# Attention with row maxima over 1024 keys at once, two banks for the transposed scores, and projection pieces in every step

## What is computed

```
x = x + attention(layernorm(x))
    q, k, v = proj(w_q), proj(w_k), proj(w_v)       # heads of 16 channels
    scores = q k^T / sqrt(16)                       # 1024 x 1024 for each of 64 (batch, head)
    out = softmax(scores) v
    out @ w_o^T
x = x + ffn(layernorm(x))                           # 512 -> 1376 (gate, up) -> 512, int4 / int8 rounding
```

## Time and profile before

| | us |
|---|---|
| median of 3 runs | 1142.4 |
| lowest and highest run | 1142.07, 1145.83 |
| the profiled execution, its own time | 1141.39 |
| its span | 1139.6 |
| PE busy | 1051.8 (92%) |
| DVE busy | 884.5 (78%) |
| ACT (ScalarE) busy | 738.2 (65%) |
| POOL (GpSimd) busy | 143.3 (13%) |
| ramp, first score to first transposed score | 66.4 to 137.2 |
| superunits 1 to 7, to the last value sum of each | 137.2 to 815.3 |
| superunit 8 | 815.3 to 900.9 |

### The profile page before, as it was taken

One profiled execution on the slowest core, in us unless ns is written; L12 is line 12 of the kernel. 1 busy time (PEld: TensorE's weight loads), 2 busy tenths in 40 slices (PEclk: granted clock), 3 DMA queues, 4 the chain that ended last, 5 costly groups with the idle time before them and its releaser, 6 DMA issues.

```text
span 1139.6 us, 18560 instructions
## 1 busy us (share of the span) xinstructions
PE 1051.8 (92%) x6882; PEld 354.3 (31%) x6882; DVE 884.5 (78%) x1573; ACT 738.2 (65%) x885; POOL 143.3 (13%) x282
## 2 busy tenths in 40 slices
PE   4889999999999999999999999999998669888886
PEld 2333222222222222222222222222222235444543
DVE  3265588988988897898888889889997267788874
ACT  4631277766777776776677677667778536656664
POOL 2200011011101201201110110111000021111210
PEclk9889999999999999999999999999999979999998
DMA  9430013102202300230220121022253251111110
GB/s 349 153 86 1 1 31 78 33 20 66 58 18 66 66 11 20 66 65 10 76 57 13 35 73 41 20 66 57 96 154 85 62 152 37 39 37 37 37 46 28
DMA packets 43862, 69.63 MB, mean 61 GB/s; under 512 B 3334, under 2 KB 21766, under 8 KB 43526
## 3 DMA queue, kind: packets, MB, share of 16 engines
q1 hardware_dynamic: 43782, 68.56, 21.6%
HBM read 46.99 MB, written 21.23 MB: 60 GB/s over the span
## 4 chain that ended last, share of the span: by engine, by line
PE 64%; DVE 12%; ACT 5%; issue 5%; DMA 5%; POOL 2%; SPq 1%; DVEq 0%; POOLq 0%; ACTq 0%
PE ps L360 20%; PE ps L312 17%; PE ps L297 10%; PE ps L341 8%; PE ps L275 4%; DVE mx L765 3%; PE ps L421 2%; ACT PB L571 2%; DMA QK<-parts_d 2%; DVE hm L860 2%; POOL rstd L1027 1%; DMA parts_d<-spl 1%; PE ps L443 1%; DVE bst L808 1%; DVE PB L806 1%
## 5 line engine op out<-in xcount | busy, mean ns | idle before, releaser
L765 DVE TENSOR_REDUCE mx<-ps 128x1 f32<-128x512 f32 x1024 | 653.3, 685 | 122.6 <-PE ps L312 116.8
L571 ACT ACTIVATE PB<-ps 128x1024 f32<-128x1024 f32 x512 | 522.5, 1024 | 196.5 <-PE ps L341 191.2
L312 PE MATMUL ps<-QK 48*128 48x512 f16 x1024 | 354.6, 385 | 11.4 <-DVE mx L765 8.2
L360 PE MATMUL ps<-PB,Vg 128*32 128x256 f32 (+1 forms) x3192 | 303.2, 451 | 8.7 <-ACT PB L571 4.6
L341 PE MATMUL ps<-QK 50*128 50x512 f16 x1024 | 300.4, 382 | 1.2 <-DMA QK<-nmT 1.1
L312 PEld LDWEIGHTS ps<-QK 48*128 48x128 f16 x1024 | 92.4, 92 | 431.3 <-DVE mx L765 379.6
L297 PE MATMUL ps<-XV,wqk 128*128 128x512 f32 x256 | 144.4, 656 | 0.0
L360 PEld LDWEIGHTS ps<-PB,Vg 128*32 128x32 f32 x3192 | 63.5, 107 | 110.9 <-issue 97.6
L421 PE MATMUL ps<-tu,Vg 128*128 128x344 bf16 x256 | 49.1, 315 | 24.6 <-DVE XV L849 24.6
L275 PE MATMUL ps<-wv,XV 128*128 128x512 f32 x128 | 69.4, 649 | 0.0
L399 PE MATMUL ps<-wo,XV 128*128 128x512 f32 x128 | 61.1, 622 | 6.0 <-DVE PB L806 5.2
(11 more groups left out here) (117 smaller groups left out, 657.7 us busy)
## 6 DMA issues: line engine op xcount, KB each, us to landing
parts_d<-spl SPq DMA_DIRECT2D x64, 128.0 KB
QK<-parts_d SPq DMA_DIRECT2D x32, 256.0 KB, 5.1
att_d<-OS SPq DMA_DIRECT2D x32, 256.0 KB
PB<-x SPq DMA_DIRECT2D x28, 256.0 KB, 2.9
QK<-parts_d SPq DMA_DIRECT2D x32, 128.0 KB, 4.7
XV<-att_d SPq DMA_DIRECT2D x2, 2048.0 KB, 8.4
QK<-rden_d SPq DMA_DIRECT2D x8, 512.0 KB, 7.8
out<-PB SPq DMA_DIRECT2D x16, 256.0 KB, 2.0
```

Source lines behind the costliest of these rows:

```text
L312: nc.tensor.matmul(ps[:, 4 + at % 2, :], QK[rows, sup % 2, 2 * set_ + p, 0, half * HALF + qt * P:half * HALF + (qt + 1) * P], QK[rows, sup ...
L360: last = nc.tensor.matmul(ps[32 * h:32 * h + 32, 6, part * n:part * n + n], Vg[:, set_, kt, h, :], PB[:, step % 2, h, part * n:part * n + ...
L571: nc.scalar.activation(PB[:, step % 2, 2 * pair:2 * pair + 2, :], ps[:, 2 * pair:2 * pair + 2, :], ACT.Exp, scale=exp_reg).then_inc(probs, 1)
L765: nc.vector.tensor_reduce(mx[:, unit % 2, qt * 4 + head, kh:kh + 1], ps[:, 4 + at % 2, :], AX.X, ALU.max)\
```

## The change

- A maximum is taken over 1024 keys in one instruction: an item is now two score matmuls into two neighbouring banks (banks 0 and 1, or 2 and 3) and one reduction of 128 x 1024, negated. A unit has 16 items in place of 32, a step two in place of four; the joining reduction and its buffer are gone.
- Transposed scores have two banks (4 and 5). Each head's matmul is followed by its own exponential of 512 columns, so a step has four exponentials in place of two. A transposed-score matmul waits for the exponential of the matmul before the last.
- PB has three buffers, in turn over all 256 steps.
- Jobs are numbered 0 to 31, k ahead of q, and run one job per unit: steps 0 to 6 of each unit carry one whole matmul and then six halves of 256 columns, step 7 none. Five jobs run ahead of the value projection in place of four, and the loop does 27 in place of 28.
- The value sum is always one piece, at the end of the step.
- In the ramp an item (two score matmuls) follows every second value matmul.
- The DMAs that stack q and k are cut into k, first half of q and second half of q, each with its own semaphore.

```diff
         def step_items(step):
-
             found = []
-            for j in range(4):
-                n = (step + AHEAD) * 4 + j
-                found.append((n // 128, n % 128 // 32, n % 32))
+            for j in range(2):
+                n = (step + AHEAD) * 2 + j
+                found.append((n // (4 * UNIT_ITEMS), n % (4 * UNIT_ITEMS) // UNIT_ITEMS, n % UNIT_ITEMS))
             return found
...
+        def job_in(sup, step):
+
+            n = 4 * sup + 5 + step // KEYT
+            return n if n < JOBS else None
...
-            last = nc.tensor.matmul(ps[:, job_bank(sup, job), :], wqk[:, qk, k, :], xT(region, k, half * HALF, HALF),
-                                    start=(k == 0), stop=(k == KT - 1))
-            if k == KT - 1:
+            last = nc.tensor.matmul(ps[:, job_bank(n), col:col + cols], wqk[:, qk, k, :],
+                                    xT(region, k, half * HALF + col, cols),
+                                    start=(k == 0 and col == 0), stop=(k == KT - 1 and col + cols == HALF))
+            if k == KT - 1 and col + cols == HALF:
                 last.then_inc(job_psum, 1)
...
-            if sup > 0 or step > 0:
-
-                pe.wait_ge(probs, sup * (2 * STEPS) + (2 * step + p - 1))
-            for side in range(2):
-                rows = slice(side * SIDE, side * SIDE + AUG)
-                last = nc.tensor.matmul(ps[:, 2 * p + side, :],
-                                        QK[rows, sup % 2, 2 * set_ + p, 1, kt * P:(kt + 1) * P],
-                                        QK[rows, sup % 2, 2 * set_ + p, 0, half * HALF:(half + 1) * HALF],
-                                        start=True, stop=True)
-            last.then_inc(st_psum, 1)
+                    pe.wait_ge(v_copy, TILES)
+            if n >= 2:
+                pe.wait_ge(probs, n - 1)
+            rows = slice(side * SIDE, side * SIDE + AUG)
+            nc.tensor.matmul(ps[:, 4 + i % 2, :],
+                             QK[rows, sup % 2, 2 * set_ + p, 1, kt * P:(kt + 1) * P],
+                             QK[rows, sup % 2, 2 * set_ + p, 0, half * HALF:(half + 1) * HALF],
+                             start=True, stop=True).then_inc(st_psum, 1)
...
             for step in range(STEPS):
-                jobs = not last and step < 16
-                item(step, 0)
+                job, r = job_in(sup, step), step % KEYT
+                item(step, 0, 0)
                 pe_scoresT(pe, sup, step, 0)
-                item(step, 1)
+                item(step, 0, 1)
+                pe_scoresT(pe, sup, step, 1)
+                if job and r == 0:
+                    pe_job(pe, job, 0)
+                elif job and r < 7:
+                    pe_job(pe, job, (r + 1) // 2, (r - 1) % 2 * (HALF // 2), HALF // 2)
+                item(step, 1, 0)
+                pe_scoresT(pe, sup, step, 2)
+                item(step, 1, 1)
+                pe_scoresT(pe, sup, step, 3)
                 if step > 0:
-                    pe_av(pe, sup, step - 1, 0, 1 if jobs else 2)
-                item(step, 2)
-                pe_scoresT(pe, sup, step, 1)
-                item(step, 3)
-                if jobs:
-                    pe_job(pe, sup + 1, region, step // 4, step % 4)
-                elif step > 0:
-                    pe_av(pe, sup, step - 1, 1, 2)
+                    pe_av(pe, sup, step - 1)
...
-                    if t >= RAMP_TILE and item < 4 * AHEAD:
-                        pe_scores(pe, 0, item // 32, item % 32)
+                    if t >= RAMP_TILE and k % 2 == 1:
+                        for kh in range(2):
+                            pe_scores(pe, 0, item // UNIT_ITEMS, item % UNIT_ITEMS, kh)
                         item += 1
...
-            nc.scalar.activation(PB[:, step % 2, 2 * pair:2 * pair + 2, :], ps[:, 2 * pair:2 * pair + 2, :],
+            nc.scalar.activation(PB[:, at % 3, 2 * (i % 2) + i // 2, :], ps[:, 4 + i % 2, :],
                                  ACT.Exp, scale=exp_reg).then_inc(probs, 1)
...
                 act_exp(act, sup, step, 0)
                 act_exp(act, sup, step, 1)
-                if step % KEYT == 0 and step > 0:
+                if step % KEYT == 1 and step > 1:
                     act_sums(act, sup, step // KEYT - 1)
-                if not last and step < 16 and step % 4 == 3:
-                    act_job(act, sup + 1, step // 4)
+                if step % KEYT == 7 and job_in(sup, step):
+                    act_job(act, job_in(sup, step))
+                act_exp(act, sup, step, 2)
+                act_exp(act, sup, step, 3)
                 if last and step in (12, 14, 16, 18):
                     act_abs(act, 2, (step - 12) // 2)
...
-            nc.vector.tensor_reduce(mx[:, unit % 2, qt * 4 + head, kh:kh + 1], ps[:, 4 + at % 2, :], AX.X, ALU.max)\
-                .then_inc(s_used, 1)
...
+            nc.vector.tensor_reduce(nm[:, unit % 2, idx:idx + 1], slot_of(at).rearrange("p a n -> p (a n)"), AX.X, ALU.max,
+                                    negate=True).then_inc(s_used, 1)
```

More of the change, by code:

```diff
@@ L1056, in _ @@
             g.tensor_tensor(rnorm[:], sqtot[:], expo[:, 0:2], ALU.pow).then_inc(wn_pow, 1)
[L1057 to L1058 removed]
+            for job in range(5):
+                pool_split_job(pool, job)
             rstds(2)
```

296 lines of the change are left out of this document (160 added, 136 removed).

## The result

The changed kernel is 0.8% slower: median 1148.95 us of 14 runs (1146.65 to 1158.33) against 1141.48 of 14 runs of the kernel before on the same chip, a ratio of 1.0076 with a 95% interval of 1.0057 to 1.0096. The forecast was 1135.5. The profiled execution took 1147.72 us, with a span of 1145.9.

The account below looks back on a forecast made before the run. PE was taken to bound steps with a job, DVE those without. Superunits -8.7, last superunit +10.9 and ramp -9.3 gave -7.1 on 1141.39, so 1134.3; the median stands 1.0 above, forecast 1135.5 us, range 1122 to 1160.

Parts of the forecast that it names:

- The maxima: Reductions over 1024 keys on DVE: 1.16 us each, 2.3 a step in place of 2.5; DVE no longer sets the pace.
- The ring: Each step: first transposed score (T0), its exponential (E0), the second exponential, fourth transposed score (T3), value sum, next T0; 2.88 us.
- The first rival: Exponentials in the ring don't overlap, each starting when the one before ends: +27 us, 1162 us; chance 0.2.
- The superunits: The six changed superunits take 95.8 us each for 97.05; with the first superunit and a saved job, -8.7 us.
- The ramp: Before the first transposed score: paired scores -6.8 us, with shorter waits, clock and a fifth early job together -9.3.
- the fifth job's 3.4: In the ramp: a fifth job ahead of the value projection adds four f32 matmuls, +3.4 us.
- The last superunit: It has no jobs, so the ring costs there: 96.6 us for 85.66, +10.9.
- rival two: The clock still falls in the ramp: +3.4 us, 1139 us; chance 0.2.
- T0: First of a step's four transposed scores on PE; from its start to E0's start 0.43 us.
- E0: First of a step's four exponentials on ACT, taken from T0; the second starts 0.48 to 0.49 us after it.
- T3: Fourth transposed score of a step on PE, waiting for the second exponential; from its start to the value sum 0.32 us.
- the fixed cost of a short exponential: Skill page's 0.57 us per 512-column exponential, against 0.48 between starts; as start to start, ring 0.09 longer.

Follow-up runs that it names:

- experiment 3: Changed kernel with the value sum between the second and third transposed score and the job's piece at the step's end; 1202.7 us, one run.
- experiment 4: Changed kernel with the value sum over only 256 of its 512 queries, half that work left out; 1114.0 us, one run.
- experiment 9: Changed kernel with the value sum in two pieces of 256 queries in the last superunit only; 1146.00 us, 1.0045 of the kernel before.
- Experiment 6: Kernel before with one edit, ramp scores in pairs after every second value matmul; 1131.70 us, 0.9917 of the kernel before.
- experiment 10: Changed kernel with three transposed-score banks from step 24 of superunit 6, four from step 21 of the last; 1123.71 us, 0.9835 of the kernel before.
- experiment 1: Changed kernel with four extra unread score matmuls in each of the last eleven steps; 1138.10 us, 0.9968 of the kernel before.
- experiment 7: Changed kernel with the value sum in two pieces throughout and ACT's copy of the sums ahead of the step's first exponential; 1186.74 us, 1.0412.
- experiment 2: Changed kernel with a third bank for transposed scores in the last superunit; 1131.15 us, 0.9908 of the kernel before.
- experiment 5: Kernel before with each 1024-column exponential cut into two of 512, all four transposed-score banks kept; 1145.91 us, 1.0026 of the kernel before.
- experiment 8: Experiment 7 with three transposed-score banks from the last superunit's first step and four from its step 21; 1191.6 us, uneven.
- experiment 11: Experiment 10 with experiment 9's edit, the value sum in two pieces in the last superunit; 1144.92 us, 1.0029 of the kernel before.
- experiment 12: Experiment 1 with experiment 9's edit, the value sum in two pieces in the last superunit; 1134.62 us, 0.9929 of the kernel before.

## Why the prediction was wrong

- **The maxima** were right: 1.22 us each, DVE no longer the pace.
- **The ring** was right to 0.01 us, with every link: 2.88 to 2.89 in steps with a half job piece and in steps of the last superunit. Experiments 3, 4 and 9 changed a link and got the step that the sum of the links gives. The first rival fell: exponentials of 0.597 start about 0.49 apart, two of them in 1.09:

```profile
311.11 1.09 ACT L593 ACTIVATE PB<-ps 128x512 f32<-128x512 f32 x2 [0.63 <-PE ps L366]
```

- **The superunits** were right in kind, 0.45 us too low each (96.25 for 95.8). The steps at a unit's edge took 3.09 + 3.29 + 3.15 = 9.53 for 9.46 computed; the rest was not traced further.
- **The ramp**: -8.9 for -9.3. Experiment 6 confirms the sum: -12.1 without the fifth job, for -12.7 computed, and the 3.2 between the two runs is the fifth job's 3.4. The gain of pairing and that of the clock were not measured apart.
- **The last superunit** is the step that failed. "Sum 96.6, so +10.9" took every step at 2.4 GHz, without a reason given for it. To the value sum at 873.30 it holds: 72.3 us for about 72.4. Behind that the sum was short by 10.2 us, all of it clock. The profile before gave no warning in so many words, as PEclk was 1.00 in these steps; but it could have been asked what PE does in a ring of 2.88 when neither scores nor jobs fill it. Its own work there is four transposed scores and a value sum, at most 1.96 us by experiment 10. I treated waiting time on PE as neutral once the ring was priced, and rival two looked for the clock only in the ramp.
- The ring at the lower clock shows the mechanism. Only PE's links grow: T0 to E0 0.64 for 0.43, T3 to the sum 0.53 for 0.32, the sum 1.87 for 1.00, with the exponentials as before. 0.64 + 0.485 + 0.594 + 0.06 + 0.53 + 1.87 = 4.18. The lower clock makes PE look busy (22.69 of 24 us), so its busy share hides the idle time that was there before the clock fell. The Trainium skill, "TensorE: Matmul & The Clock Gate", "What's actually happening", says that the clock follows how busy the array has lately been; experiment 1 agrees, as more work alone took 10.9 us off. The busy share of a trace is not that measure, though: experiment 9 has PE at 12.00 of 12 us and the clock at 1.2 GHz.
- On the fixed cost of a short exponential, what the prediction quotes of small tiles is said by the Trainium skill, "VectorE: DVE Perf Modes", section on the TRN2 errata, of operands in SBUF; the exponentials here read PSUM.
- Two small slips of the sum: 7.5, 1.0 and 0.3 make 8.8 where it says 8.7, and 1134.3 with 1.0 added is 1135.3 where it says 1135.5. They change nothing.

Without those 10.2 us the profile would stand 6.3 - 10.2 = -3.9 us from the kernel before, which is where experiment 1 stands (0.9968 of 1143.0 is -3.7). The other 3 us between -7.1 and -3.9 are mostly the 0.45 in each of six superunits. Ring and clock together outweighed a ramp that was really won.

## What to carry to other kernels

When a buffer count falls, add up the ring of waits that each engine's order closes through the fewer buffers, and do it for every stretch: the part where other work fills the ring pays little, the part where that work has run out pays all of it, and may lose TensorE's clock on top. Take resources back as soon as their owner is done (banks 7 and 0 here), and time the independent parts of a large change one by one: here the ramp alone gave 0.8%, and the rest of the change took more than that away. Work that is moved from one ring may close another, as the mirror ring of experiments 3, 4 and 7 did.

## What the hardware showed that was not expected

- The clock of TensorE against the pace of its work, in the scoreless steps. With four transposed scores and one whole value sum in a step, it held 2.4 GHz at steps of 1.96 us (experiment 10) and of 2.39 (experiment 2), and stood at 1.2 GHz where the ring of 2.88 left it idle. With the sum in two pieces it held at 2.14 (experiment 5), and in 2.46 it held until a wait of 1.54 us came (experiment 9), and to the end where that wait was 0.27 (experiment 7, profiled execution). A long wait isn't needed, though: experiment 8 lost the clock with no idle time over 0.84 us in the 10 us ahead. And the same kernel differs from one execution to the next, by 15 us in experiment 7. What decides is open.
- Once down, it needn't come back when PE is busy without a gap: 0.50 from 880 to 904 in experiment 9, with PE at 12.00 of 12 us. Within a superunit, where scores follow, it does come back (experiment 11, pieces 1.11 apart again from 856.28 on). Once the clock had fallen in the scoreless steps of the last superunit it stayed down to their end, in the changed kernel and in experiments 8, 9 and 11. Added work (experiments 1 and 12) and more banks with the sum in one piece (2 and 10) kept it up there; four banks with the sum in two pieces (8 and 11) did not.
- 512 columns of an f32 value sum cost 1.00 us to the next instruction's start, 256 cost 0.57: a cut in two adds 0.14.
- Two 512-column exponentials from PSUM are 0.597 long each, and the second starts about 0.49 behind the first (four in 2.07, 810.94 in experiment 2). The Trainium skill, "VectorE: DVE Perf Modes", in its section on the TRN2 errata, has 0.57 for one by its formula; as a distance between starts the rows here contradict it by 0.08.
